# An RNN and an LSTM in one loop: GpSimd makes the high halves of the recurrent LSTM weights

## The reference, cut to what matters

```python
# x (32, 128, 512), h0 = cond_1024 (32, 512), all float32
# RNN:   Wx, Wh (512, 512);  LSTM: Wx, Wh (512, 2048)
def _L0_cond_ref(x, h0, Wx, Wh, b):
    xW = einsum('ntd,dh->nth', x, Wx) + b
    def step(prev_h, xw):
        next_h = tanh(prev_h @ Wh + xw)
        return next_h, next_h
    ...
def _L1_cond_ref(x, h0, Wx, Wh, b):
    xW = einsum('ntd,dg->ntg', x, Wx) + b
    def step(carry, xw_t):
        prev_h, prev_c = carry
        a = xw_t + prev_h @ Wh
        i, f, o = sigmoid(a[:, :H]), sigmoid(a[:, H:2*H]), sigmoid(a[:, 2*H:3*H])
        g = tanh(a[:, 3*H:])
        next_c = f * prev_c + i * g
        next_h = o * tanh(next_c)
        return (next_h, next_c), next_h
    ...
x = x + _L0_cond_ref(x, cond_1024, ...)
x = x + _L1_cond_ref(x, cond_1024, ...)
```

## Time and profile before

| | |
|---|---|
| median of 3 executions | 850.23 us (849.87 to 851.4) |
| profiled execution | its span alone is given: 847.5 us |
| TensorE busy | 830.7 us, 98% |
| VectorE, ScalarE, GpSimd busy | 660.3, 582.7 and 337.6 us |
| granted TensorE clock | full in all slices |

### The profile page before, as it was taken

How to read it: one execution, slowest core, us unless ns; L and a number is a source line. 1 busy time by engine, 2 the same in 40 slices (tenths; PEclk the granted TensorE clock), 3 DMA queues, 4 the chain that set the end, 5 groups by cost and what they waited for, 6 DMA issues and landing times.

```text
span 847.5 us, 52211 instructions
## 1 busy us (share of the span) xinstructions
PE 830.7 (98%) x22860; PEld 621.8 (73%) x22860; DVE 660.3 (78%) x1830; ACT 582.7 (69%) x1596; POOL 337.6 (40%) x697
## 2 busy tenths in 40 slices
PE   7999999999999999999999999999999999999996
PEld 4665556687777877777777787777777777777885
DVE  3579688788887877888778887888878887777765
ACT  4896477777676777766767776676777677677642
POOL 1212466834334343443444434344343443434320
PEclk9999999999999999999999999999999999999999
DMA  8801100111001111100111100011110000000000
GB/s 319 267 19 27 29 15 16 28 29 29 17 17 30 29 29 29 29 10 23 29 29 29 29 21 20 22 29 29 29 28 17 17 17 17 17 15 17 16 15 18
DMA packets 40196, 30.71 MB, mean 36 GB/s; under 512 B 5772, under 2 KB 38688, under 8 KB 38688
## 3 DMA queue, kind: packets, MB, share of 16 engines
q1 hardware_dynamic: 39712, 27.27, 11.2%
q10 hardware_dynamic: 256, 0.11, 0.0%
HBM read 18.95 MB, written 8.39 MB: 32 GB/s over the span
## 4 chain that ended last, share of the span: by engine, by line
PE 93%; DVE 3%; ACT 2%; DMA 1%; issue 1%; SPq 0%; ACTq 0%; DVEq 0%
PE ps_l L1279 35%; PE ps_l L1345 28%; PE ps_r L1422 9%; PE ps_r L1442 9%; PE ps_l L1323 4%; PE ps_l L1292 2%; PE ps_l L1312 2%; PE ps_r L1404 1%; PE ps_r L1393 1%; DMA whr_raw<-in_L_cond_Wh 1%; PE ps_l L1238 1%; DVE pre_l L1080 0%; PE ps_l L1266 0%; ACT gates L795 0%; PE ps_l L1256 0%
## 5 line engine op out<-in xcount | busy, mean ns | idle before, releaser
L496 POOL TENSOR_TENSOR xb<-xb,h_l 128x128 f32<-128x128 f32 x127 | 58.0, 457 | 420.3 <-DVE h_lo L1126 414.2
L1345 PE MATMUL ps_l<-whl_raw,wxl_raw 128*32 128x256 f16 x3888 | 125.2, 273 | 1.7 <-ACT wxl_raw L700 1.3
L1345 PE MATMUL ps_l<-wxl_hi,wxl_raw 128*32 128x256 f16 x2592 | 124.6, 273 | 0.0
L1279 PE MATMUL ps_l<-whl_hi,hT_hi 128*32 128x512 f16 x1888 | 123.5, 379 | 1.1 <-DVE hT_hi L1110 1.1
L1279 PE MATMUL ps_l<-whl_hi,hT_lo 128*32 128x512 f16 x1888 | 123.3, 379 | 0.0
L1279 PE MATMUL ps_l<-whl_lo,hT_hi 128*32 128x512 f16 x1888 | 123.3, 379 | 0.0
L1345 PEld LDWEIGHTS ps_l<-whl_raw,wxl_raw 128*32 128x32 f16 x3888 | 104.0, 97 | 15.8 <-ACT ps_l L681 2.7
L795 ACT ACTIVATE gates<-pre_l 128x256 f32<-128x256 f32 x108 | 45.1, 417 | 101.5 <-DVE pre_l L1080 101.5
L1279 PEld LDWEIGHTS ps_l<-whl_hi,hT_lo 128*32 128x32 f16 x1888 | 51.9, 97 | 50.3
L1279 PEld LDWEIGHTS ps_l<-whl_lo,hT_hi 128*32 128x32 f16 x1888 | 51.9, 97 | 50.3
L1080 DVE SCALAR_TENSOR_TENSOR pre_l<-ps_l,g_products,wxl_raw 128x256 f32<-128x256 f32 x108 | 47.5, 480 | 48.3 <-PE ps_l L1279 43.6
(11 more groups left out here) (178 smaller groups left out, 1936.4 us busy)
## 6 DMA issues: line engine op xcount, KB each, us to landing
xb<-in_x SPq DMA_DIRECT2D x128, 64.0 KB, 2.2
out<-xb SPq DMA_DIRECT2D x124, 64.0 KB, 1.8
whl_raw<-in_L_cond_Wh SPq DMA_DIRECT2D x4, 1024.0 KB, 6.4
wxl_raw<-in_L_cond_Wx SPq DMA_DIRECT2D x4, 1024.0 KB, 5.9
wxr_raw<-in_L_cond_Wx SPq DMA_DIRECT2D x1, 1024.0 KB, 5.6
whr_raw<-in_L_cond_Wh SPq DMA_DIRECT2D x1, 1024.0 KB, 7.7
out<-xb SPq DMA_DIRECT2D x4, 48.0 KB, 1.6
wxl_raw<-peaks SPq DMA_DIRECT2D x5, 2.0 KB, 1.9
```

Of the source, the lines that this page charges most:

```text
L496: nc.gpsimd.tensor_tensor(xb[g % NX][:, t, :], xb[g % NX][:, t, :], h_l[s % 2][:, :], ALU.add).then_inc(out_done, 1)
L1279: last = nc.tensor.matmul(ps_l[s % 4][quarter(j), :], (hT_hi, hT_lo)[h_part][:, k, :], gate_slice(whl[w_part][k], j), start=False, stop=(h ...
L1345: last = nc.tensor.matmul(at[quarter(j), :], stationary, weights[:, j, :, :], start=False, stop=(y_part == 1 and k == 1), skip_group_check ...
```

## The change

GpSimd makes the four high halves of the recurrent LSTM weights (`whl_high`), chunks 0 and 1 at the end of its tick 5, chunks 2 and 3 at the end of its tick 6, behind the adds of the tick. ScalarE no longer makes them. On ScalarE the four bounds of the input weights stand in ticks 5, 6, 6 and 7 instead of 6, 7, 7 and 8. VectorE's, TensorE's and SyncE's programs stay as they are.

```diff
-        W_BOUND_AT = {1: [(OF_H, 0)], 2: [(OF_H, 1)], 3: [(OF_H, 2)], 4: [(OF_H, 3)], 6: [(OF_X, 0)], 7: [(OF_X, 1), (OF_X, 2)], 8: [(OF_X, 3)]}
-        W_HIGH_AT = {5: [(OF_H, 0)], 6: [(OF_H, 1), (OF_H, 2)], 7: [(OF_H, 3)], 9: [(OF_X, 1), (OF_X, 2)], 10: [(OF_X, 3)]}
+        W_BOUND_AT = {1: [(OF_H, 0)], 2: [(OF_H, 1)], 3: [(OF_H, 2)], 4: [(OF_H, 3)], 5: [(OF_X, 0)], 6: [(OF_X, 1), (OF_X, 2)], 7: [(OF_X, 3)]}
+        W_HIGH_AT = {9: [(OF_X, 1), (OF_X, 2)], 10: [(OF_X, 3)]}
+        POOL_HIGH_AT = {5: [0, 1], 6: [2, 3]}
         W_HIGH_LATE_AT = {8: [(OF_X, 0)]}
...
+            def whl_high(k):
+                pool.wait_ge(w_step[OF_H], W_STEPS)
+                nc.gpsimd.tensor_scalar(whl[0][k][:, :], whl_raw[k][:, :], w_scale[:, OF_H:OF_H + 1], None,
+                                        ALU.mult).then_inc(w_high[OF_H], 1)
+
             for k in range(END):
...
                 if k < T:
                     add_yT(k)
                     add_y(k)
+                for chunk in POOL_HIGH_AT.get(k, []):
+                    whl_high(chunk)
```

## The result

| | before | after |
|---|---|---|
| median | 850.05 us of 4 runs (848.86 to 851.4) | 858.67 us of 4 runs (857.76 to 860.0) |
| ratio | | 1.0109, interval 1.0096 to 1.0123 |
| profiled execution | span 847.5 us | time 860.0 us, span 858.2 us |

The ratio is the one on record, not exactly the quotient of the two medians. The 860.0 us of the profiled execution are the upper end of its four; its time stands 1.8 us above its span, as in every other execution whose two numbers are known. GpSimd's chunk is L587.

What follows compares the result with a forecast made beforehand. TensorE, busy 98% of the span, bounds the kernel. VectorE and GpSimd taking turns at 2.0 us a chunk add 4.6 us to the 847.5 us span; with 2.7 us around it, 854.8 us, range 850.1 to 861.0 us.

Steps and rivals of the forecast that it cites:

- the likeliest case's own range: Whole kernel: VectorE and GpSimd take turns at 2.0 us a chunk, 853.2 to 855.8 us; chance 0.50.
- the rival with a chunk of 3.3 us: GpSimd's multiply is slower, by the select with the memset's start: sum 9.8 us, 860.0 us; chance 0.14.
- What bounds the kernel: Ticks 5 to 8: TensorE busy 44.85 of 45 us; ScalarE's time worth nothing, VectorE's may cost once its lead is used.
- The price of a chunk: GpSimd's one-input multiply of 2048 columns: 0.19 us to start plus 0.875 ns a column, about 2.0 us.
- Exclusion: VectorE and GpSimd exclude each other on operations with two inputs in SBUF and take turns; price 4.6 us.
- The rival without it: One-input GpSimd chunks don't exclude VectorE, so TensorE stays full: 850.2 us; chance 0.10.
- the one in which VectorE keeps its turn: VectorE holds its turn while it has work; LSTM's transposed h 1.1 us late, 851.3 us; chance 0.10.
- the rule of 4 us for each us of a chunk: Each us by which a GpSimd chunk exceeds 2.0 adds 4 us, as all four lie in the chain.
- the stall of tick 6: TensorE waits for the RNN's transposed h, ready at 37.1 but wanted at 35.88 us: 1.2 us, contained in the 4.6.
- Who waits first: TensorE takes the LSTM's transposed h at 44.49 us before; it now starts at about 49.1, 4.6 us late.
- Covered by 1.9 us, so there is no third stall: The RNN's transposed h, ready about 54.1 us, comes before TensorE wants it at 56.0 us; nothing more is lost.
- the 2.7 us: Median of the runs, 850.23 us, above the profiled span of 847.5 us; left unchanged in the forecast.

Runs made afterwards that it cites:

- pool_only: Changed kernel with ScalarE's bounds of the input weights back in ticks 6, 7, 7 and 8; GpSimd still makes the four high halves: 859.78 us, ratio 1.0109.
- price: Kernel before plus three GpSimd multiplies alone ahead of the loop (2048 and 1024 columns to float16, 1024 to float32): 848.17 us, one run.
- beside_read: Kernel before plus four idle GpSimd multiplies in the chunks' places, results unused, ScalarE still making the high halves: 859.02 us, ratio 1.0101.
- beside_write: Kernel before plus four times three GpSimd memsets of 2048 float16 columns in the chunks' places, reading nothing: 852.64 us, ratio 1.0044.
- x_first: Changed kernel with VectorE's transpose of x in tick 7 moved ahead of the first cell: 858.54 us, ratio 1.0114.
- fill: Changed kernel with 24 useless TensorE matmuls in tick 7, ahead of the product that waits for the transpose of x: 859.0 us, ratio 1.0106.
- three_fill: Changed kernel with 24 useless TensorE matmuls in tick 7 and chunk 3 back on ScalarE: 854.97 us, ratio 1.0058.
- pool_last_two: Changed kernel with only chunks 2 and 3 on GpSimd; ScalarE makes 0 and 1 in ticks 5 and 6: 853.62 us, ratio 1.0047.
- pieces: Changed kernel with each GpSimd chunk split into eight operations of 256 columns: 869.21 us, ratio 1.0227.
- bounds_only: Kernel before with only ScalarE's bounds of the input weights one tick earlier; ScalarE keeps the high halves: 851.84 us, ratio 1.0028.
- pool_first_two: Changed kernel with only chunks 0 and 1 on GpSimd; ScalarE makes 2 and 3 in ticks 6 and 7: 851.86 us, ratio 1.0033.
- after_h: Changed kernel in which GpSimd's chunk 2 waits for h of the LSTM's first step: 862.04 us, ratio 1.0156.

## Why the prediction was right in direction and too small in size

It said 854.8 us, range 850.1 to 861.0 us, and slower at 0.74. The median is 858.67 us: in the range, outside the likeliest case's own range, 8.6 instead of 4.6 us more. That it falls into the range at all is luck: it lies near the rival with a chunk of 3.3 us (860.0), and no chunk took 3.3 us. By its steps:

- **What bounds the kernel**: right that VectorE's lead is what the change eats, and that ScalarE's time is worth nothing or close to it (`pool_only` leaves 1 us open).
- **The price of a chunk** failed, and with it most of the sum. It took 2.0 us with ends at 1.88 and 4.4; it is 5.44 (`price`), above both. The row taken as the nearest, a select of 128 columns, gave no slope, only one length; the split into start and slope was chosen by me, at the low end. The select with the memset's start gave 1.57 ns a column; measured are 2.54. Nor was the two-input add a bound from above: nothing but its having one input more spoke for it. The Trainium skill, "GPSIMD Engine Reference", calls one-input work roughly line rate in "Engine selection", which the runs contradict (2.54 ns a column, where two inputs take 2.06); the estimate from its best case in "Elementwise", 3.1 us, is too low as well.
- **Exclusion** is right: `beside_read` shows it without any wait for a result. The rival without it (0.10) and the one in which VectorE keeps its turn (0.10) fall, though in `beside_read` VectorE did keep its turn once, over two low halves. (That transposes keep 0.42 us beside GpSimd's work was read from a row with nothing beside it, at 33.35 us; after the change the one at 37.63 us, beside chunk 1, takes 0.41.) The Trainium skill, "SBUF — State Buffer", "SBUF: two separate sides", limits the lock against a VectorE operation with two SBUF inputs to a GpSimd operation that reads SBUF; `beside_write` agrees, its rows keep 2.59, 2.3 and 0.29 us. It also has the lock held for the whole instruction; here VectorE gets through earlier, see below.
- **How long a turn holds**: the prediction added the operation's whole length. Measured is 3.3 to 3.7 us from a chunk of 5.44 us or more. Had the price alone been right, the rule of 4 us for each us of a chunk would have given 4.6 + 4 x 3.44 = 18.4 us, and 868.6 us is outside the range. Two mistakes of opposite sign are in the 4.6.
- **Who is held**: chunk 1 was to hold the RNN's low parts once more; they got in before it, so the stall of tick 6 is 0.5, not 1.2 us. Chunk 2 held the cell's sum, where the prediction had i x g; chunk 3 held the low halves 2 and 3 and not the sum.
- **Who waits first**: the h of the LSTM, said the prediction, at 44.49 us. It was the transpose of x, which stands ahead of h in VectorE's tick 7 and is needed by the product just before (L1393 in the kernel before). The list of who waits for what had no entry for it. `x_first` shows that it doesn't matter for the time, only for where the wait is seen.
- **"Covered by 1.9 us, so there is no third stall"** failed. The prediction held VectorE's delay against TensorE's next need only, and took the pauses from 74 us on to hang on TensorE's own products, as they do in the trace of before. After the change the chain runs through VectorE from 31.8 to 89.2 us and meets TensorE in tick 12: the RNN's h at 60.0 us, the scale of `OF_X` at 65.0, ScalarE's high halves, the wait for the high half of h. With the clock kept up (`fill`) the third stall is visible, 1.24 us.
- **The clock** was not foreseen: 5.2 us of standing still are followed by about 6 us at half clock. It is 2.94 us on TensorE's account, and `fill` shows that it is worth nothing here.
- **Around the span** 1.8 us belong. The other 0.9 of the 2.7 us are what the profiled execution of before lay under the median of its runs; for a forecast of a median the 2.7 us were right, and no part of the miss.

What sets the 8.6 us is VectorE's account: 13.5 us more of holding, 4.4 us of it in idle time that it had, 9.05 us left. Where the chain runs through VectorE it follows the runs: +9.1 in `pool_only` for 10.0 us measured, +9.0 in `fill` for 9.2, +8.9 in `x_first` for 9.4, +8.7 in `beside_read` for 9.2, +5.6 in `three_fill` for 5.5, +3.9 in `pool_last_two` for 4.2, +18.6 in `pieces` for 19.8. In `bounds_only` and `pool_first_two` it agrees too (+2.3 for 2.1, +2.5 for 2.7), but by chance, since the chain there is the load's. Two runs are 2 us off, `beside_write`, as said above, and `after_h` (+10.9 for 12.9): there TensorE, behind its 6.45 us of waiting and at the lower clock, comes to the LSTM's step 2 11.2 us later than before, counted from the scale, so its own chain is the longer one, and 1.4 us lie ahead of the scale.

## What to carry to other kernels

Price an operation that no row shows by running it alone before it is trusted; one length of a relative is no slope, and "fewer inputs" is no upper bound. When an engine off the critical path is held, add up what it is given and take off the idle time between two fixed points of its own program: what is left moves everything behind the second point, though the waits of the bound engine name other tiles. A longest wait, or a stretch at a low clock, is worth only what no second chain beside it covers; filling it, or reordering in front of it, tells. And before a run's loss is put down to what was changed in it, follow its own chain: an account that gives the right number can still lie beside it, as in `pool_first_two`.

## What the hardware showed that was not expected

- GpSimd's multiply by a column of scales costs 2.54 ns a column and 0.24 us to start (5.44, 2.84 and, in pieces of 256 columns, 0.92 us), the same with float16 and float32 output, and more than its two-input add at 2.06 ns.
- Exclusion doesn't last as long as the operation. The first low part of the RNN's weights needs 1.26 us and took 4.59 from 31.80 us, so it was held until 35.1 us: 3.5 us after chunk 0 started (31.59) and 1.9 us before it ended (31.59 + 5.45). The sum of the cell was held until 3.7 us after the start of chunk 2, the low half 2 until 3.5 us after that of chunk 3. No row says what GpSimd does in the rest.
- The hold can go the other way, and for more than one operation: in `beside_read` a low half that started 0.02 us ahead of a chunk kept its length, the next low half too, and the chunk took 9.79 us. In `pool_last_two` chunk 2, started beside a low half, took 7.53 us.
- Memsets on GpSimd (2048 columns of float16, 11.20 us for six, 22.4 us in all) hold no VectorE operation with two inputs.
- After 5.2 us without work TensorE ran at 0.50 of its clock for about 6 us, and after a pause of 2.5 us (`bounds_only`) at 0.67 in the mean of the following 5.1 us, partly at either level (products of 1061 and of 592 ns); where work filled the pause the clock stayed at 1.00.
